# The last 128 steps of a recurrence, each cut into two halves of 64 columns with a PSUM bank of its own

## What is computed

```python
x = x + attention(x, cond_1024, ...)            # 16 heads, causal, softmax, output projection
h = cond_1024                                   # (8, 512)
xw = einsum('ntd,dh->nth', x, Wx) + b
for t in range(512):
    h = tanh(h @ Wh + xw[:, t])                 # one step: (8, 512) @ (512, 512)
    hs[:, t] = h
x = x + hs
```

## Time and profile before

| | |
|---|---|
| median of 3 runs | 1801.43 us (1799.96 to 1805.03) |
| the profiled execution's own time | 1800.27 us |
| its span, first to last instruction | 1798.5 us |
| mean granted TensorE clock | 0.967 |
| TensorE matmul busy / weight load busy | 1634.6 us (91%) / 1378.1 us (77%) |
| VectorE / ScalarE / GpSimd busy | 888.8 / 709.9 / 149.6 us |
| first tanh of the tail to its last tanh | 1525.46 to 1789.46 us |

### The profile page before, as it was taken

One profiled execution on the slowest core, in us unless ns is written; L12 is line 12 of the kernel. 1 busy time (PEld: TensorE's weight loads), 2 busy tenths in 40 slices (PEclk: granted clock), 3 DMA queues, 4 the chain that ended last, 5 costly groups with the idle time before them and its releaser, 6 DMA issues.

```text
span 1798.5 us, 67877 instructions
## 1 busy us (share of the span) xinstructions
PE 1634.6 (91%) x29292; PEld 1378.1 (77%) x29292; DVE 888.8 (49%) x2986; ACT 709.9 (39%) x2205; POOL 149.6 (8%) x248
## 2 busy tenths in 40 slices
PE   5788889898999998999999999898998998999997
PEld 4777778786878787877878788686886887887876
DVE  4444435454545455555555565465655574222222
ACT  2444545444344444444444444444444453111111
POOL 0110100010000100010111100011001000000000
PEclk8988989999999999999999999998998999999999
DMA  7744536443435464554545566554565561100000
GB/s 253 188 146 138 145 118 186 131 129 108 127 111 155 109 160 119 141 150 126 138 128 154 131 160 159 137 151 132 139 157 136 153 152 38 27 16 17 26 16 21
DMA packets 228442, 221.67 MB, mean 123 GB/s; under 512 B 22952, under 2 KB 187048, under 8 KB 227632
## 3 DMA queue, kind: packets, MB, share of 16 engines
q1 hardware_dynamic: 211568, 175.86, 37.0%
q0 software_dynamic: 16576, 41.46, 8.1%
HBM read 141.45 MB, written 75.76 MB: 121 GB/s over the span
## 4 chain that ended last, share of the span: by engine, by line
PE 72%; DVE 9%; DMA 7%; issue 5%; ACT 4%; SPq 2%; POOL 1%; DVEq 0%; POOLq 0%; ACTq 0%
PE rec L926 24%; PE turned L849 8%; PE dense L381 7%; PE dense L382 6%; PE dense L383 6%; PE pv L862 4%; PE scores L841 4%; PE scores L926 3%; PE dense L897 3%; DVE pre L753 3%; ACT hist L594 3%; DMA msk<-mask 2%; DMA x_dram<-x1nat 2%; PE pv L880 2%; DVE probs L688 1%
## 5 line engine op out<-in xcount | busy, mean ns | idle before, releaser
L926 PE MATMUL rec<-wh,hist 128*8 128x128 f32 x14336 | 483.7, 275 | 62.9 <-ACT hist L594 56.6
L926 PEld LDWEIGHTS rec<-wh,hist 128*8 128x8 f32 x14336 | 355.2, 94 | 145.5 <-ACT hist L594 103.9
L552 ACT ACTIVATE probs<-probs,nmax 128x128 f32<-128x128 f32 (+3 forms) x512 | 287.9, 563 | 220.6 <-DVE nmax L688 211.7
L594 ACT ACTIVATE hist<-pre 128x32 f32<-128x32 f32 x512 | 131.9, 258 | 576.7 <-DVE pre L763 340.4
L688 DVE CUSTOM_DVE_ANT_0 probs<-scores,msk,nimg 128x128 f32<-128x128 f32 (+3 forms) x512 | 276.2, 544 | 58.4 <-PE scores L841 56.5
L753 DVE STREAM_TRANSPOSE pre<-rec 128x128 f32<-128x128 f32 x448 | 141.3, 315 | 319.8 <-PE rec L926 317.4
L849 PE MATMUL turned<-ident,probs 128*128 128x128 f32 x1280 | 241.0, 288 | 1.9 <-DVE probsT L697 0.9
L841 PE MATMUL scores<-kq 96*128 96x128 f32 (+3 forms) x512 | 203.8, 403 | 37.7 <-DVE nmax L688 23.7
L849 PEld LDWEIGHTS turned<-ident,probs 128*128 128x128 f32 x1280 | 145.3, 141 | 65.3 <-issue 55.2
L697 DVE COPY probsT<-turned 128x128 f32<-128x128 f32 (+3 forms) x256 | 124.7, 487 | 97.0 <-PE turned L849 95.8
L559 ACT COPY probsT<-turned 128x128 f32<-128x128 f32 (+3 forms) x256 | 108.1, 422 | 147.9 <-PE turned L849 146.7
(11 more groups left out here) (119 smaller groups left out, 2293.1 us busy)
## 6 DMA issues: line engine op xcount, KB each, us to landing
kq<-kq_dram SPq DMA_DIRECT2D x96, 320.0 KB, 5.6
kq<-kq_dram SPq DMA_DIRECT2D x96, 256.0 KB, 4.7
kq<-kq_dram SPq DMA_DIRECT2D x96, 192.0 KB, 3.7
kq_dram<-qs_hi SPq DMA_DIRECT2D x128, 128.0 KB, 2.5
kq_dram<-ks_hi SPq DMA_DIRECT2D x128, 128.0 KB, 2.4
kq<-kq_dram SPq DMA_DIRECT2D x96, 128.0 KB, 2.6
xin<-x SPq DMA_DIRECT2D x32, 256.0 KB, 3.2
kq_dram<-qs_lo SPq DMA_DIRECT2D x64, 128.0 KB, 2.4
```

Of the source, the lines that this page charges most:

```text
L552: act.activation(probs[:, g % PROBS, 0:n], probs[:, g % PROBS, 0:n], ACT.Exp, scale=-1.0, bias=nmax[:, e, h:h + 1], accum_out=rowsum[:, e, ...
L594: act.activation(hist[:, g // HALF % 2, :, :, g % HALF], pre[:, :, 0:B], ACT.Tanh).then_inc(h_ready, 1)
L926: last = pe.matmul(d[Q * j:Q * j + B, 0:P], hist[:, before // HALF, f, :, before % HALF], wh[:, f, P * j:P * j + P], start=f == 0 and not ...
```

## The change

Only the tail is changed (`g >= FIRST`, step 384 on). The 128 columns of a bank become two halves of 64 (in each group j, columns 0 to 64 and 64 to 128), the first in `scores[t % 2]`, the second in `turned[t % 2]`. On TensorE each product of 128 columns becomes two of 64: first the `wx` products of both halves, then four groups of 8 `wh` products, in the order contraction chunks 0 and 1 for the first half, for the second half, then chunks 2 and 3 for the first half, for the second half. The chunks 0 and 1 of h are the ones that come out of the first half, so the first two groups wait for the first tanh only, the last two for the second. VectorE transposes and adds in two pieces, ScalarE does two tanh of 128x16. The semaphores `rec_ready`, `rec_turned`, `pre_ready` and `h_ready` count halves from step 384 on.

```diff
+        def half_banks(t):
+
+            return scores[t % 2], turned[t % 2]
+
+        def halves_done(t):
+
+            return t + 1 + max(t + 1 - FIRST, 0)
...
+                        for k in range(2):
+                            part = slice(2 * k, 2 * k + 2)
+                            act.wait_ge(pre_ready, halves_done(g - 1) + k + 1)
+                            act.activation(hist[:, g // HALF % 2, part, :, g % HALF], pre[:, part, 0:B], ACT.Tanh
+                                           ).then_inc(h_ready, 1)
...
-                    dve.transpose(pre_all, rec_bank(g)[:, 0:P]).then_inc(rec_turned, 1)
-                    dve.wait_ge(rec_turned, g + 1)
                     if b == BLOCKS - 1:
-                        dve.tensor_tensor(pre[:, :, 0:B], pre[:, :, 0:B],
-                                          bx[:].unsqueeze(2).broadcast_to([P, C, B]), ALU.add).then_inc(pre_ready, 1)
+                        for k in range(2):
+                            part = slice(2 * k, 2 * k + 2)
+                            done = halves_done(g - 1) + k + 1
+                            dve.wait_ge(rec_ready, done)
+                            dve.transpose(pre_all[:, 2 * Q * k:2 * Q * k + 2 * Q], half_banks(g)[k][:, 0:2 * Q]
+                                          ).then_inc(rec_turned, 1)
+                            dve.wait_ge(rec_turned, done)
+                            dve.tensor_tensor(pre[:, part, 0:B], pre[:, part, 0:B],
+                                              bx[:, part].unsqueeze(2).broadcast_to([P, 2, B]), ALU.add
+                                              ).then_inc(pre_ready, 1)
...
-                        pe.wait_ge(rec_turned, g - 1)
-                        for f in range(C):
-                            for j in range(C):
-                                pe.matmul(d[Q * j:Q * j + B, 0:P], x1step[:, half, f, :, g % HALF],
-                                          wx[:, f, :].rearrange("p (a j c) -> p a j c", a=C, j=C)[:, :, j, :],
-                                          start=f == 0, stop=False)
...
+                elif kind == "step":
+                    before = (g - 1) % STEPS
+                    half = g // HALF % 2
+                    cols = P // 2
+                    if g % HALF == 0:
+                        pe.wait_ge(x1_set_out, (g - FIRST) // HALF + 1)
+                    if g > FIRST + 1:
+                        pe.wait_ge(rec_turned, halves_done(g - 2))
+                    for part, d in enumerate(half_banks(g)):
+                        for f in range(C):
+                            for j in range(C):
+                                pe.matmul(d[Q * j:Q * j + B, 0:cols], x1step[:, half, f, :, g % HALF],
+                                          wx[:, f, :].rearrange("p (a j c) -> p a j c", a=C, j=C)
+                                          [:, 2 * part:2 * part + 2, j, :], start=f == 0, stop=False)
+                    for k, part in ((0, 0), (0, 1), (1, 0), (1, 1)):
+
+                        d = half_banks(g)[part]
+                        if part == 0:
+                            pe.wait_ge(h_ready, 1 + halves_done(g - 1) - (1 - k) * (g > FIRST))
+                        for f in (2 * k, 2 * k + 1):
+                            for j in range(C):
+                                last = pe.matmul(d[Q * j:Q * j + B, 0:cols],
+                                                 hist[:, before // HALF, f, :, before % HALF],
+                                                 wh[:, f, P * j + cols * part:P * j + cols * part + cols],
+                                                 start=False, stop=f == C - 1)
+                        if k == 1:
+                            last.then_inc(rec_ready, 1)
```

More of the change, by code:

```diff
@@ L372, in heads_tile @@
             return kq_tiles[:, group % TILES, 0:HC * n].rearrange("p (j n) -> p j n", j=HC)
-        def rec_bank(t):
-            return scores[0] if t >= (BLOCKS - 1) * P and t % 2 == 0 else rec
+        FIRST = (BLOCKS - 1) * P
+        def half_banks(t):
+            return scores[t % 2], turned[t % 2]
+        def halves_done(t):
+            return t + 1 + max(t + 1 - FIRST, 0)
         def split_product(out, hi, lo, moving_hi, moving_lo, first, last):
@@ L590, in _ @@
                 elif kind == "step":
-                    act.wait_ge(pre_ready, g + 1)
                     if g % HALF == 0 and g >= 2 * HALF:
                         wait_dense(act, "out", g // HALF - 2, 0)
-                    act.activation(hist[:, g // HALF % 2, :, :, g % HALF], pre[:, :, 0:B], ACT.Tanh).then_inc(h_ready, 1)
+                    if g < FIRST:
+                        act.wait_ge(pre_ready, g + 1)
+                        act.activation(hist[:, g // HALF % 2, :, :, g % HALF], pre[:, :, 0:B], ACT.Tanh
+                                       ).then_inc(h_ready, 1)
+                    else:
+                        for k in range(2):
+                            part = slice(2 * k, 2 * k + 2)
+                            act.wait_ge(pre_ready, halves_done(g - 1) + k + 1)
+                            act.activation(hist[:, g // HALF % 2, part, :, g % HALF], pre[:, part, 0:B], ACT.Tanh
+                                           ).then_inc(h_ready, 1)
         @block.vector
@@ L760, in _ @@
                     else:
+                        dve.wait_ge(rec_ready, g + 1)
+                        dve.transpose(pre_all, rec[:, 0:P]).then_inc(rec_turned, 1)
+                        dve.wait_ge(rec_turned, g + 1)
                         cells = xw[:, :, r, :, :, s] if b % 2 == 0 else xw[:, r, :, :, :, s]
@@ L906, in _ @@
                     last.then_inc(dense_ready, 1)
-                elif kind == "step":
+                elif kind == "step" and g < FIRST:
                     before = (g - 1) % STEPS
[L909 to L914, removed]
-                        pe.wait_ge(rec_turned, g - 1)
-                        for f in range(C):
-                            for j in range(C):
-                                pe.matmul(d[Q * j:Q * j + B, 0:P], x1step[:, half, f, :, g % HALF],
-                                          wx[:, f, :].rearrange("p (a j c) -> p a j c", a=C, j=C)[:, :, j, :],
-                                          start=f == 0, stop=False)
-                    elif g == 0:
+                    if g == 0:
                         pe.wait_ge(weights_loaded, WEIGHT_LOADS)
@@ L925, in _ @@
                         for j in range(C):
-                            last = pe.matmul(d[Q * j:Q * j + B, 0:P], hist[:, before // HALF, f, :, before % HALF],
-                                             wh[:, f, P * j:P * j + P], start=f == 0 and not tail, stop=f == C - 1)
+                            last = pe.matmul(rec[Q * j:Q * j + B, 0:P], hist[:, before // HALF, f, :, before % HALF],
+                                             wh[:, f, P * j:P * j + P], start=f == 0, stop=f == C - 1)
@@ L929, in _ @@
                 elif kind == "out":
-                    pe.wait_ge(h_ready, (g + 1) * HALF + 1)
+                    pe.wait_ge(h_ready, 1 + halves_done((g + 1) * HALF - 1))
                     for f in range(C):
```

1 line of the change is left out of this document (removed).

## The result

The changed kernel takes 2022.22 us, median of 4 runs (2011.36 to 2029.34). The kernel before, run beside it, takes 1803.23 us (1799.96 to 1807.91). The ratio is 1.1213, with an interval of 1.1182 to 1.1244: slower by 12%. The prediction was 2010 us, with a range of 1950 to 2070.

What follows compares the result with a forecast made beforehand. Before, a 2.02 us tail ring with TensorE nearly full; after, instruction supply at 3.7 us per 256. Tail 476 us against 266 adds 210 us to 1800, giving 2010 us, range 1950 to 2070.

Steps and rivals of the forecast that it cites:

- The ring: Tail: the step's chain of wh products, transposition, sum and tanh, read as 2.02 us a step before the change.
- 64 columns should take about half: TensorE in the tail: a half-width product starts some 13 ns after the last, so 128 take 1.66 to 1.8 us.
- The paced pairs: Rival, tail: each LDWEIGHTS and MATMUL pair costs 25.8 ns whatever its columns; 3.3 us a step, 1964 us; chance 0.07.
- the ring alone: Tail step with the halves overlapped and nothing else holding it up: 1.79 us for 2.02, 28 us less over 128 steps.
- pieces that don't shrink: Tail: if halved VectorE and ScalarE work stays full length, 0.15 us a step is added and 9 us of gain remain.
- Supply: Tail: TensorE's instructions come in packets of 256, 3.7 us each; a step needs one, 476 us in all, 210 us added.
- four standstills: Tail before the change: TensorE stops mid-burst behind "issue" four times for 0.17 to 0.40 us, read as late instruction packets.
- the chain: Tail instruction fetch, one link at a time: 1.1 us to packet start, 1.13 its length, 1.5 landing to use; 3.7 us.
- the two other links: Tail instruction fetch: entering a block to the next packet's start, 1.1 us, and landing to use, 1.5 us.
- The rival that rested on that, 1773 us: Rival, tail: several instruction blocks are under way, supply stays hidden, the array sets 1.8 us a step; chance 0.11.
- The clock: Rival, tail: TensorE, half busy, falls to 1.2 GHz; at most 0.4 us a step more, 2060 us; chance 0.10.
- Before step 384 nothing moves: Everything ahead of the tail: the change adds or saves no time there.

Runs made afterwards that it cites:

- the small products: Kernel before with 16 added products of 8 columns in each tail step, into an idle bank, 192 TensorE instructions a step; 1903.09 us, ratio 1.0559.
- the kernel with wide products: Changed kernel with the 32 input products of a tail step replaced by 4 of 512 columns that nobody reads, 144 instructions a step; 1811.27 us, ratio 1.0061.
- the count alone: Kernel before with only each tail product cut in two of 64 columns, same bank and order, 256 instructions a step; 2016.65 us, ratio 1.119.
- the dose from 144 to 256 instructions: Four kernels with 144, 192, 256 and 256 TensorE instructions a step; tails 271.9, 363.6, 479.6 (products cut in two) and 475.8 us (the change).

## Why the prediction was right

**Ring and array.** The ring's length of 2.02 us was as in the trace of before. "64 columns should take about half: some 13 ns from start to start" held: 14 ns in the group of 32, and 16 start in 1702.27 - 1702.04 = 0.23 us. The paced pairs, "25.8 ns whatever its columns", are refuted by the same rows and by the 8 ns of the small products. The Trainium skill ("TensorE: Matmul & The Clock Gate", section "Back-to-back issue gap") has a floor of 25 ns there; in this kernel, whose neighbouring products go to different column groups, the trace has 14 and 8 ns, and the measurement decides.

**Overlap.** Predicted 1.79 us for the ring alone, 1.75 measured where nothing held it up. The pieces were as forecast (transposition 0.25 and 0.24, sum 0.17, tanh two in 0.60). But the size is right partly by luck, because another path sets it. I had summed the path through the second tanh and the third group of products, with the second transposition behind the first sum's end; it starts 0.09 us after that sum's start. So this path is shorter: in the free step of the kernel with wide products the third group starts at 1640.58, the transposition at 1641.05, and the second tanh ends at 1641.54 + 0.60 = 1642.14, 1.56 us in all. The path through the first tanh, which I had not summed, is the longer one: the first group at 1640.13, three groups up to the first half's result and its transposition at 1641.05, first tanh, next first group at 1641.88, 1.75 us. The 0.15 us for pieces that don't shrink was summed wrongly: the prediction's own pieces give 2 x (0.32 - 0.25) + 2 x (0.19 - 0.17) + 0.01 = 0.19 us, so 5 us would be left and not 9, and the time of that case would be 1796 us and not 1792. "If nothing else stood against the change, it would give 1773 us" stays untested as a whole, since every kernel with the change's two banks was bound by the supply.

**Supply.** This was the step on which all hung, read from four standstills of 0.17 to 0.40 us. "3.7 us for 256 instructions": 3.74 measured. The "476 us" were for 128 steps; the 127 intervals between tanh took 475.8, which is 480 for 128. That it came so near is partly luck. With each packet's own length the chain was 1.32 + 1.6 + 1.1 = 4.0, 1.47 + 1.5 + 1.5 = 4.5 and 1.12 + 1.3 + 1.1 = 3.5 us at three of the four places, and 3.7 came of taking the mean length and one restart. Of the 3.75 us a packet in the tail, 1.08 are its length, and 2.67 are left for the two other links, where 2.6 was taken. It was the count that did it (479.6 us with the count alone), as the dose from 144 to 256 instructions shows. The links by themselves were seen at one place of the changed kernel (0.9 to 1.1 us to the packet's start, 1.28 for its length, 1.2 to 1.5 from landing to use), and lie near the four of before. That each of the links is fixed by itself was not tested, and why the next packet is not asked for earlier no run shows. The Trainium skill ("Runtime: NRT & Kernel Launch", section "Instruction fetch mechanics") says that the crossing to the next block is mostly hidden. The block of 256 is right here; hidden it is only as long as a block lasts more than some 3.8 us, and in the stretches read the packets show one block ahead, never several. The rival that rested on that, 1773 us, is refuted.

**"With 3.7 us a step the overlap on VectorE and ScalarE is worth nothing":** shown, 475.8 us with it and 479.6 without. The 3.8 us between them are 0.03 us a step; by one profiled execution each that isn't told from scatter.

**The clock.** Given 0.10, on top of the supply, "at most 0.4 us a step". It was there and small: 0.95 over the tail, where before had 1.00. A window that shows it, rows inside it, and the DMA view from 1889 to 1905 us in slices of 0.4 us:

```profile
1891.00:1901.00 10.00, 7.66 (x287) 7.10 (x278) 2.34 (x10) 0.92 (x4) 0.00 (x0) 0.50 0.02 4
```

```profile
1895.32 1.04 PE L950 MATMUL scores<-wx,vbuf 128*8 128x64 f32 x32 [0.91 <-DVE vbuf L658]
...
1898.70 1.08 PE L950 MATMUL scores<-wx,vbuf 128*8 128x64 f32 x32
```

```profile
GB/s 0 0 0 0 41 0 0 0 0 0 0 0 0 0 0 41 0 0 0 0 0 0 0 0 41 0 0 20 0 0 0 0 0 0 41 0 0 0 0 42
```

Ten microseconds at 1.2 GHz (0.50 granted). The 128 MATMUL of a step take 1898.70 - 1895.32 = 3.38 us there, as the 2 x 1.7 of the prediction had it. Packets of 16 KB read 41 GB/s in such a slice. They start at 1890.6, 1895.0, 1898.6 and 1902.6, 4.0 us apart on the mean, where the tail's mean is 3.75. A part of this isn't the clock's, since TensorE also waits 0.91 us for the input to be set out. Such stretches are few, and no cost of theirs shows in the tail as a whole: with the products cut in two and nothing else it was granted 0.98 and took 479.6 us, and the change with 0.95 took 475.8.

**"Before step 384 nothing moves":** no instruction does, but the profiled execution was 15 us late there, and the runs reach from 2011 to 2029 us. The medians differ by 219 us, where 210 were forecast for 128 steps and the tail shows 212 over 127 intervals. The 7 us between are within that scatter, and no run assigns them.

## What to carry to other kernels

Count the instructions of TensorE, not only its columns: divide the time of a stretch by its LDWEIGHTS and MATMUL together, and where it comes near 3.8 us for 256 of them, cutting products smaller costs time however well it overlaps. A few short standstills behind "issue" whose distance is a multiple of 256 instructions are the sign that the supply is at its limit already, even if they cost 0.1% of the time. Look for the overlap in what waits (here the first chunks of the next step waiting for the first tanh alone), which costs no instruction on the full engine.

## What the runs showed of the hardware

- The supply of TensorE's instructions: 3.74 to 3.82 us for 256 in four kernels that it bounds, about 14.8 ns an instruction. At 128 columns and 2.4 GHz a pair of LDWEIGHTS and MATMUL takes 25.8 ns of the array, but 2 x 14.8 = 29.6 ns of the supply; the kernel before escapes it in the tail because its ring gives a pair 2.02 / 64 us, or 31.6 ns.
- Small products into changing column groups start 8 ns (8 columns) and 14 ns (64 columns) apart.
- VectorE lets a transposition begin 0.09 us after the start of an independent sum of 0.17 us ahead of it: in the rows they overlap.
- Weights of 32 columns, or one more wait ahead of the burst, cost 0.08 us a step in a ring; taking work from TensorE lowered its clock (0.96 for 1.00) and gave back 5 us of what was saved.
